# A reordered opening in a two-layer kernel: idle products, moved SiLUs, evictions and decays, and a new spread of the key units

## The chip, the cores and the metric

The kernel runs on one core of one Trainium2 chip. The metric is the device time of one execution in microseconds (us); three runs were taken. The engines are TensorE (PE in the rows), VectorE (DVE), ScalarE (ACT), GpSimd (POOL) and SyncE (SP), which issues most of the transfers.

## The reference, cut to what matters

The reference is a network of two layers on x (4 batches, 512 tokens, width 512) and a context (4, 512, 256). Layer 0 is a selective scan on the context, gated by the normalised x, and then a feed-forward with quantised activations and ternary weights. Layer 1 is cross-attention with 16 heads and a mixture of experts. What this change touches is the scan of batch 0, the ternary weights and the attention's keys:

```python
# the scan (one batch): e = 512 channels, n = 16 states
x  = in_proj_w @ ctx                          # product A
u  = silu(conv4(x) + conv_b)                  # 4-tap convolution along time
dt_lo, Bm, Cm = split(x_proj_w @ u)           # product B
delta = softplus(dt_proj_w @ dt_lo + dt_proj_b)    # product C
for n in range(16):
    state_n[t] = state_n[t-1] * exp(delta[t] * A[:, n]) + delta[t] * u[t] * Bm[n, t]
y  = sum_n state_n * Cm[n] + D * u
out = y * silu(z)                             # z is the normalised x

# ternary weights of the feed-forward
scale = clip(mean(abs(w), axis=-1), 1e-5); w_q = clip(round(w / scale), -1, 1)

# keys of the attention, per head
k = rmsnorm((ctx @ Wk).reshape(B, S, H, D), gk)
```

## The kernel before, in words

Every engine runs a queue of its own in the order of the code, and all waits are semaphores that are written by hand. The program has an opening and then a loop over the four batches ("turns"). Inside a turn the scan of the next batch is interleaved with the feed-forward and the attention of this one, and TensorE is busy nearly throughout. The opening has nothing to interleave with, so it takes in work that belongs to later turns.

**The head of the opening.** `scan_a` makes product A in four parts (TensorE), and ScalarE copies each from PSUM to `xin`. The convolution of channels 0 and 1 is made on TensorE (`scan_conv`) with diagonal matrices that GpSimd builds (`diagonals`), and that of channels 2 and 3 on VectorE (`taps`). ScalarE applies SiLU: `scan_silu` to a bank of PSUM, `summed_silu` to a result of `taps`. `scan_b` and `scan_c` make products B and C. In C's four banks ScalarE reads each twice, once for `Abs` and once for `Identity` with the offset `dt_b`; two banks of PSUM serve the four parts in turn. The softplus then goes back and forth: an exponential and a logarithm on ScalarE, five passes on VectorE (`softplus_start`, `softplus_end`). Ahead of `softplus_start` in VectorE's queue stands `gate_norm`, whose power function is GpSimd's (`rstd`). GpSimd's queue has, in this order, `diagonals(0)`, a `partition_all_reduce` of the gains, and that power.

**The eight rounds.** The 16 states are scanned in eight rounds r of two (i = 0 and 1). In each, VectorE multiplies by B (`times_b`), scans four times (`scans`), then multiplies both states by C (`times_c`), and works out the signs of one block of weights (`ternary(r + 2)`, none in rounds 6 and 7). ScalarE makes the factors exp(delta * A) of the next round, one call of four instructions per state: `decay(0, r + 1, i)`. TensorE adds the results into four banks, `y_sum(r, i)`. `times_b(r + 1, 1)` overwrites what `y_sum(r, 1)` reads and waits for it, and `scans` waits for its decay.

**What fills the rounds.** A key unit n is two heads of the keys of one batch. On TensorE it is `first_k(n, h)` (four products of 512 columns, each two records in the trace) and `first_sums(n, h)` (sums of squares). On ScalarE it is `first_out(n)` (four instructions: two squares, two scaled copies) and `first_sums_out(n, h)`. SyncE loads the next weights and stores the unit (`k_dma`). A ternary block r is `w_sums` (four sums of absolute values, ScalarE), `ternary` (VectorE), `tern` (transposes on TensorE) and `w_out` (five evictions on ScalarE). Units 0 and 1 stand ahead of the rounds (`U_EARLY = 2`), `round_units(r)` gives the units of round r (two in rounds 0 to 4, one in 5 to 7), and unit 15, the first of the turn, stands behind the rounds. `y_first` is the set of banks that `y_sum` adds to; it is begun with D * u (`d_times_u`).

## Time and profile before

| | |
|---|---|
| median of 3 runs | 1937.62 us (1936.42 to 1937.79) |
| the profiled execution's own time | 1934.49 us |
| its span | 1932.8 us |
| TensorE busy | 1797.8 us (93%) |
| VectorE busy | 1206.4 us (62%) |
| ScalarE busy | 1090.6 us (56%) |
| mean granted TensorE clock | 0.970 |

The span runs from the first to the last instruction, so 1.7 us of the profiled execution's time lie outside it. The shares are means over the whole span. The opening takes its first 240 us, and the shares there differ from those of the turns.

### The profile page before, as it was taken

How to read it: one execution, taken by the hardware profiler on the slowest of the kernel's cores; microseconds unless marked ns; L12 is line 12 of the kernel's file. 1: busy time of each engine (PE TensorE's matmuls, PEld its weight loads, DVE VectorE, ACT ScalarE, POOL GpSimd, SP SyncE). 2: the span in 40 equal slices, each digit the busy share in tenths (PEclk: the TensorE clock that was granted, in tenths of full speed). 3: DMA queues.
4: the chain of work that ended last, by engine and by line, in shares of the span. 5: the costliest groups of instructions: out<-in, count | busy, mean ns of one | idle time of the engine just before them, and what ended most of it. 6: DMA issues, size and time to landing. Idle time of an engine off the chain costs nothing.

```text
span 1932.8 us, 26062 instructions
## 1 busy us (share of the span) xinstructions
PE 1797.8 (93%) x8318; PEld 1154.4 (60%) x8319; DVE 1206.4 (62%) x1551; ACT 1090.6 (56%) x2454; POOL 236.1 (12%) x197
## 2 busy tenths in 40 slices
PE   7799899999999999999999999998989999989895
PEld 3455455776765576767655777765567676634442
DVE  5799778877775788777678977783641001144422
ACT  5577447666654676666547666754554554453420
POOL 0002011110100010000102000000031010033032
PEclk9799899999999989999999999999999999999997
DMA  7165222323231122223122323232044323213433
GB/s 213 44 191 189 88 57 66 93 76 94 83 84 61 51 87 89 91 77 102 50 88 66 93 76 103 76 120 77 33 137 90 78 68 85 49 50 108 127 105 124
DMA packets 113862, 175.76 MB, mean 91 GB/s; under 512 B 12400, under 2 KB 65648, under 8 KB 113280
## 3 DMA queue, kind: packets, MB, share of 16 engines
q1 hardware_dynamic: 99136, 158.06, 26.0%
q0 software_dynamic: 13840, 15.21, 3.9%
q10 hardware_dynamic: 816, 1.57, 0.2%
q8 instruction: 42, 0.69, 0.1%
q14 instruction: 28, 0.23, 0.0%
HBM read 146.23 MB, written 34.87 MB: 94 GB/s over the span
## 4 chain that ended last, share of the span: by engine, by line
PE 78%; DVE 9%; ACT 6%; issue 4%; another core or an unknown queue 2%; DMA 1%; POOL 1%; SPq 1%; ACTq 0%; DVEq 0%
PE ps L1942 27%; PE pp L1942 17%; PE px L1942 17%; PE pd L1942 6%; PE po L1942 5%; DVE arena L1469 2%; PE ps L2136 1%; PE pp L2290 1%; DVE arena L1461 1%; ACT hbuf L1235 1%; PE pd L2261 1%; PE po L2261 1%; ACT arena L980 1%; PE px L1994 1%
## 5 line engine op out<-in xcount | busy, mean ns | idle before, releaser
L1469 DVE TENSOR_TENSOR_SCAN arena<-arena 128x512 f32<-128x512 f32 x256 | 292.2, 1204 | 16.3 <-ACT arena L980 15.7
L1235 ACT ACTIVATE hbuf<-ps,shift,rms_k 128x512 f32<-128x512 f32 x256 | 198.4, 777 | 124.3 <-PE ps L1942 117.2
L1942 PE MATMUL ps<-qkT 128*128 128x512 f32 x512 | 250.8, 601 | 7.3 <-ACT hbuf L1235 4.0
L1942 PE MATMUL pp<-wq,xnT 128*128 128x256 f32 x1024 | 233.6, 382 | 0.0
L1942 PEld LDWEIGHTS pp<-wq,xnT 128*128 128x128 f32 x1024 | 191.6, 192 | 24.0
L813 POOL TENSOR_TENSOR rms<-ssv,minus_half 128x4 f32<-128x4 f32 x64 | 80.9, 1264 | 860.5 <-ACT ssv L1211 860.5
L980 ACT ACTIVATE arena<-arena,a_neg 128x512 f32<-128x512 f32 x256 | 163.7, 722 | 0.0
L1942 PEld LDWEIGHTS po<-v_ext,hbuf 128*128 128x128 f32 x768 | 105.9, 191 | 61.2 <-issue 61.2
L1942 PEld LDWEIGHTS ps<-qkT 128*128 128x128 f32 x512 | 82.5, 190 | 84.0 <-ACT hbuf L1235 58.2
L1461 DVE TENSOR_TENSOR arena<-arena,bc 128x2048 f32<-128x2048 f32 x56 | 126.3, 2287 | 6.7 <-issue 5.6
L1942 PE MATMUL px<-wo,oT 128*128 128x512 f32 x256 | 121.8, 596 | 5.9 <-issue 5.9
L1682 DVE TENSOR_TENSOR xc<-xc,px 128x512 f32<-128x512 f32 x64 | 43.1, 677 | 129.7 <-PE px L1942 129.7
L1480 DVE TENSOR_TENSOR arena<-arena,bc 128x2048 f32<-128x2048 f32 x52 | 118.7, 2282 | 0.0
L1942 PE MATMUL ps<-wo,oT 128*128 128x512 f32 x256 | 115.9, 593 | 1.1 <-ACT v_ext L1197 1.1
L1942 PE MATMUL ps<-wv,ctx_att 128*128 128x256 f32 x512 | 115.7, 379 | 0.0
L1229 ACT ACTIVATE qkT<-pp 128x512 f32<-128x512 f32 x64 | 37.9, 597 | 137.0 <-PE pp L2290 137.0
L1487 DVE TENSOR_TENSOR arena<-arena 128x2048 f32<-128x2048 f32 x48 | 110.0, 2292 | 6.5 <-ACT arena L972 3.2
L1942 PE MATMUL pd<-v_ext,hbuf 128*128 128x129 f32 x768 | 106.7, 275 | 0.0
L1942 PE MATMUL po<-v_ext,hbuf 128*128 128x129 f32 x768 | 106.4, 275 | 0.0
L1942 PEld LDWEIGHTS ps<-wv,ctx_att 128*128 128x128 f32 x512 | 97.3, 190 | 13.2
L1942 PE MATMUL pp<-ctx_att,wk 128*128 128x512 f32 x200 | 98.0, 635 | 2.8 <-DMA ctx_att<-in_ctxT 1.8
L1942 PE MATMUL px<-v_ext,hbuf 128*128 128x129 f32 x512 | 99.0, 275 | 0.0
(340 smaller groups left out, 3034.2 us busy)
## 6 DMA issues: line engine op xcount, KB each, us to landing
bc<-bc_dram SPq DMA_DIRECT2D x56, 512.0 KB, 5.4
wo<-in_Wo SPq DMA_DIRECT2D x32, 512.0 KB, 3.6
wq<-in_Wq SPq DMA_DIRECT2D x32, 512.0 KB, 3.5
qkT<-kt_dram SPq DMA_DIRECT2D x32, 512.0 KB, 4.4
hbuf<-in_w SPq DMA_DIRECT2D x8, 1024.0 KB, 10.0
wv<-in_Wv SPq DMA_DIRECT2D x32, 256.0 KB, 2.8
kt_dram<-xnT SPq DMA_DIRECT2D x13, 512.0 KB, 3.0
wk<-in_Wk SPq DMA_DIRECT2D x25, 256.0 KB, 3.3
```

The costliest lines, as they stand in the source:

```text
L813: nc.gpsimd.tensor_tensor(rms[:, j], ssv[:, j], half, ALU.pow).then_inc(rms_done, 1)
L980: nc.scalar.activation(dA[i][:, e], delta[:, e], ACT.Exp, scale=a_neg[:, e, bass.ds(g * GH + i, 1)]).then_inc(exp_done[i], 1)
L1229: nc.scalar.activation(qT[:, h], pp[bank][:], ACT.Copy).then_inc(pp_drained[bank], 1)
L1235: nc.scalar.activation(pT[:, h, k], ps[s_use % 2][:], ACT.Exp, bias=shift[:, 0:1], scale=rms_k[:, bass.ds(G * (GH * NT) + (h * NT + k), 1) ...
L1461: V.tensor_tensor(hb[i], du, bc_i[:, 0:1, :].broadcast_to((P, EC, L)), ALU.mult).then_inc(dbu_done[i], 1)
L1469: V.tensor_tensor_scan(hb[i][:, e], dA[i][:, e], hb[i][:, e], 0.0, ALU.mult, ALU.add).then_inc(scan_done[i], 1)
L1480: V.tensor_tensor(dst, hb[i], bc_i[:, 1:2, :].broadcast_to((P, EC, L)), ALU.mult).then_inc(hc_done[i], 1)
L1487: V.tensor_tensor(u, u, hb[i], ALU.add).then_inc(y_added, 1)
L1682: V.tensor_tensor(xc[:, k], xc[:, k], px[bank][:], ALU.add).then_inc(px_drained[bank], 1)
L1942: return nc.tensor.matmul(out, lhsT, rhs, start=first, stop=last, **kw)
L1994: m = nc.tensor.transpose(bank[:, e * P:(e + 1) * P], u[:, e, k * P:(k + 1) * P], ident[:])
L2261: m = nc.tensor.transpose(o_bank[h][:, k * P:(k + 1) * P], o_rows[:, h, k], ident[:])
```

## The change: what it does

- TensorE runs 14 products of 128 columns whose result nobody reads, ahead of its wait for the first weights (`ip_in`). `conv_w` and `ident` are loaded third and fourth, with a semaphore of their own, `conv_in`, for which GpSimd's diagonals and VectorE's taps wait in place of all constants.
- On ScalarE one SiLU stands ahead of the first set of weight sums and the other three between the two sets.
- The four banks of C are evicted by VectorE, offset added, behind its two ternary blocks; ScalarE takes the absolute value from SBUF, behind the exponential of `a_neg`. VectorE's `gains_set` moves behind the taps.
- Unit 0's evictions stand ahead of `w_out(0)`, its sums behind `decay(0, 0, 0)`; TensorE's order follows. `decay(0, 1, 0)` moves ahead of round 0, and `y_sum(0, 0)` ahead of unit 2's products.
- Rounds 0 and 7 have one key unit, the six between have two. Unit 15 is round 7's, stored from the buffer `wq`, and its part in the first turn is dropped.

```diff
         def round_units(r):
-            first = U_EARLY + r + min(r, R_TWO)
-            return range(first, first + (2 if r < R_TWO else 1))
+            first = U_EARLY + max(0, 2 * r - 1)
+            return range(first, first + (1 if r in (0, TC - 1) else 2))
...
             sp.dma_start(ipT[:], dram["ipT"].rearrange("(c p) e -> p c e", p=P)).then_inc(ip_in, 16)
+            sp.dma_start(conv_w[:], dram["conv_w"].rearrange("(e p) k -> p e k", p=P)).then_inc(conv_in, 16)
+            sp.dma_start(ident[:], dram["ident"]).then_inc(conv_in, 16)
             constants()
...
                 if s == 0:
-                    pool.wait_ge(const_in, 16 * 17)
+                    pool.wait_ge(conv_in, 16 * 2)
...
                     act.wait_ge(full, n)
-                    if s == 0:
-                        nc.scalar.activation(hb[0][:, e], bank, ACT.Abs, bias=dt_b[:, e:e + 1]).then_inc(sp_abs, 1)
                     nc.scalar.activation(delta[:, e], bank, ACT.Identity, bias=dt_b[:, e:e + 1]).then_inc(drained, 1)
+            def first_abs():
+                for e in range(EC):
+                    _, _, drained, n = at(before_turns, ("C", 0), e)
+                    act.wait_ge(drained, n)
+                    nc.scalar.activation(hb[0][:, e], delta[:, e], ACT.Abs).then_inc(sp_abs, 1)
...
-            act.wait_ge(const_in, 16 * 17)
+            act.wait_ge(const_in, 16 * 15)
+            summed_silu(0, range(2, 3))
             tern(w_sums, 0)
+            scan_silu(0, before_turns, range(1))
+            summed_silu(0, range(3, 4))
+            scan_silu(0, before_turns, range(1, 2))
             tern(w_sums, 1)
-            for e in range(2):
-                scan_silu(0, before_turns, range(e, e + 1))
-                summed_silu(0, range(2 + e, 3 + e))
             scan_b(0, before_turns)
-            scan_c(0, before_turns)
+            nc.scalar.activation(a_neg[:], a_neg[:], ACT.Exp).then_inc(a_exp, 1)
+            first_abs()
             softplus_exp(0)
-            nc.scalar.activation(a_neg[:], a_neg[:], ACT.Exp).then_inc(a_exp, 1)
             softplus_ln(0)
+            first_out(0)
             tern(w_out, 0, range(4))
             act.wait_ge(a_ready, 1)
             decay(0, 0, 0)
+            for h in range(GH):
+                first_sums_out(0, h)
             tern(w_out, 1, range(4))
             decay(0, 0, 1)
             d_times_u(0)
             tern(w_sums, 2)
-            for n in range(U_EARLY):
+            for n in range(1, U_EARLY):
                 first_out(n)
                 for h in range(GH):
                     first_sums_out(n, h)
+            decay(0, 1, 0)
...
-                    if r + 1 < TC:
+                    if r + 1 < TC and not r == i == 0:
                         decay(0, r + 1, i)
...
+            dve.wait_ge(conv_in, 16 * 2)
             taps(0, before_turns, range(2, EC))
+            gains_set()
             for r in range(2):
                 ternary(0, r, 1)
+            for e in range(EC):
+                bank, full, drained, n = at(before_turns, ("C", 0), e)
+                dve.wait_ge(full, n)
+                V.tensor_scalar(delta[:, e], bank, dt_b[:, e:e + 1], None, ALU.add).then_inc(drained, 1)
             shift_set()
             gate_norm(0, 0)
...
+            pe.wait_ge(const_set, 1)
+            for _ in range(14):
+                mm(pd[:, 0:P], ones[:], ones[:], True, True)
+            pe.wait_ge(ip_in, 16)
...
-            for r in range(2):
-                tern(r, range(4))
-            first_sums(0, 0)
-            for n in range(1, U_EARLY):
-                first_k(n, 0)
-                first_sums(n - 1, 1)
-                first_k(n, 1)
-                first_sums(n, 0)
+            tern(0, range(4))
+            for h in range(GH):
+                first_sums(0, h)
+            tern(1, range(4))
+            for h in range(GH):
+                first_k(1, h)
             pe.wait_ge(ud_done, EC)
             for e in range(EC):
                 mm(y_first[e][:], ident[:], u[:, e], True, True)
-            first_sums(U_EARLY - 1, 1)
+            for h in range(GH):
+                first_sums(1, h)
             for r in range(TC):
                 units = round_units(r)
+                if r == 0:
+                    y_sum(r, 0)
                 for h in range(GH):
                     first_k(units[0], h)
-                y_sum(r, 0)
+                if r:
+                    y_sum(r, 0)
...
-            n0 = unit_at(0, 0)[0]
-            k_turned(n0, 0, B - 1, 0)
-            k_turned(n0, 0, B - 1, 1)
-            k_sums(n0, 0, k_sq_turn, 0)
...
                     scan_a(b + 1, turn_, 0)
-                    kss(0, 1)
+                    if b:
+                        kss(0, 1)
                     scan_a(b + 1, turn_, 1)
```

The first place is the head of ScalarE's queue, behind the four copies of product A; `qk_raw,w_sum<-hbuf` are the weight sums, `arena<-ps,conv_b` and `arena<-arena,conv_b` the SiLUs. Before:

```order
L998 ACTIVATE qk_raw,w_sum<-hbuf 128x512 [waits abs_done,stage_in0,const_in]
L998 ACTIVATE qk_raw,w_sum<-hbuf 128x512 [waits abs_done] x3
L998 ACTIVATE qk_raw,w_sum<-hbuf 128x512 [waits abs_done,stage_in1]
L998 ACTIVATE qk_raw,w_sum<-hbuf 128x512 [waits abs_done] x3
L923 ACT_TABLE_LOAD
L923 ACTIVATE arena<-ps,conv_b 128x512 [waits py_full0]
L929 ACTIVATE arena<-arena,conv_b 128x512 [waits taps_done]
L923 ACTIVATE arena<-ps,conv_b 128x512 [waits py_full1]
L929 ACTIVATE arena<-arena,conv_b 128x512 [waits taps_done]
```

Of the change, at the same place:

```order
L932 ACT_TABLE_LOAD [waits taps_done]
L932 ACTIVATE arena<-arena,conv_b 128x512 [waits const_in]
L1006 ACTIVATE qk_raw,w_sum<-hbuf 128x512 [waits abs_done,stage_in0]
L1006 ACTIVATE qk_raw,w_sum<-hbuf 128x512 [waits abs_done] x3
L926 ACTIVATE arena<-ps,conv_b 128x512 [waits py_full0]
L932 ACTIVATE arena<-arena,conv_b 128x512 [waits taps_done]
L926 ACTIVATE arena<-ps,conv_b 128x512 [waits py_full1]
L1006 ACTIVATE qk_raw,w_sum<-hbuf 128x512 [waits abs_done,stage_in1]
L1006 ACTIVATE qk_raw,w_sum<-hbuf 128x512 [waits abs_done] x3
```

The last SiLU now stands ahead of the second set of sums, and the table load carries the wait for the first tap sums.

The second place is ScalarE's queue around the beginning of round 0: `ssv_k<-pp,eps` are unit 1's sums, `dsum<-pp` and `wo<-pp,kgain` unit 2's evictions, `arena<-arena,a_neg` the decays of round 1. Before:

```order
L1042 ACTIVATE ssv_k<-pp,eps 128x4 [waits pp_full0]
L1042 ACTIVATE ssv_k<-pp,eps 128x4 [waits pp_full1]
L1029 ACTIVATE dsum<-pp 128x512 [waits pp_full0]
L1034 ACTIVATE wo<-pp,kgain 128x512 [waits k_stored0]
L1029 ACTIVATE dsum<-pp 128x512 [waits pp_full1]
L1034 ACTIVATE wo<-pp,kgain 128x512
L980 ACTIVATE arena<-arena,a_neg 128x512 [waits scan_done0]
```

Of the change:

```order
L1050 ACTIVATE ssv_k<-pp,eps 128x4 [waits pp_full0]
L1050 ACTIVATE ssv_k<-pp,eps 128x4 [waits pp_full1]
L988 ACTIVATE arena<-arena,a_neg 128x512 [waits scan_done0]
L988 ACTIVATE arena<-arena,a_neg 128x512 x3
L1037 ACTIVATE dsum<-pp 128x512 [waits pp_full0]
L1042 ACTIVATE wo<-pp,kgain 128x512 [waits k_stored0]
L1037 ACTIVATE dsum<-pp 128x512 [waits pp_full1]
```

The four instructions of `decay(0, 1, 0)` now stand ahead of unit 2's evictions.

The third place is TensorE's queue there: `arena,ident` into ps, po and pd begins `y_first`, `ones,dsum` are unit 1's sums, `ctx_att,wk` unit 2's products, `xc,ident` is `y_sum(0, 0)`. Before:

```order
L1942 MATMUL pd<-arena,ident 128x512
L1942 MATMUL pp<-ones,dsum 128x1 [waits k_squares,pp_drained1]
L1942 MATMUL pp<-ones,dsum 128x1 x3
L1942 MATMUL pp<-ctx_att,wk 128x512 [waits pp_drained0,wk_in,ctx_att_in]
L1942 MATMUL pp<-ctx_att,wk 128x512
L1942 MATMUL pp<-ctx_att,wk 128x512 [waits pp_drained1,wk_in,ctx_att_in]
L1942 MATMUL pp<-ctx_att,wk 128x512
L1942 MATMUL ps<-xc,ident 128x512 [waits hc_done0]
```

Of the change:

```order
L1962 MATMUL pp<-ones,dsum 128x1 [waits k_squares,pp_drained1]
L1962 MATMUL pp<-ones,dsum 128x1 x3
L1962 MATMUL ps<-xc,ident 128x512 [waits hc_done0]
L1962 MATMUL ps<-xc,ident 128x512
L1962 MATMUL po<-xc,ident 128x512
L1962 MATMUL pd<-xc,ident 128x512
L1962 MATMUL pp<-ctx_att,wk 128x512 [waits pp_drained0,wk_in,ctx_att_in]
```

`y_sum(0, 0)` has gone ahead of unit 2's products.

## Rows read from the trace of the kernel before

**Rows 1.** Windows of the opening: length, each engine's busy time, granted TensorE clock, DMA

```profile
50.00:108.00 58.00, 45.02 (x188) 27.00 (x189) 43.19 (x45) 36.55 (x77) 0.00 (x0) 0.81 0.27 79
108.00:230.00 122.00, 107.79 (x501) 61.79 (x500) 118.93 (x88) 79.55 (x143) 13.69 (x2) 0.95 0.47 153
```

**Rows 2.** Timeline, round 1 (start, length, engine, line, instruction, idle before)

```profile
71.80 2.29 DVE L1461 TENSOR_TENSOR arena<-arena,xnT 128x2048 f32<-128x2048 f32 x1 [0.22 <-DVE qkT L1429]
...
85.34 2.55 ACT L980 ACTIVATE arena<-arena,a_neg 128x512 f32<-128x512 f32 x4
...
86.16 4.57 DVE L1469 TENSOR_TENSOR_SCAN arena<-arena 128x512 f32<-128x512 f32 x4 [12.07 <-ACT arena L980]
92.11 2.29 DVE L1461 TENSOR_TENSOR arena<-arena,xnT 128x2048 f32<-128x2048 f32 x1 [1.37 <-PE pd L1942]
...
104.08 0.17 DVE L1422 TENSOR_SCALAR w_scale<-w_sum 128x4 f32<-128x4 f32 x1 [0.69 <-ACT qk_raw L998]
```

**Rows 3.** The chain that ended last, head of the opening: start, length, what

```profile
19.08 2.56 ACT qk_raw L998 x8
...
22.96 0.69 ACT arena L923
25.70 3.62 PE ps L1942 x16
29.84 1.11 PE ps L1942 x2
...
37.26 1.92 ACT arena L960
```

**Rows 4.** Timeline of VectorE, head of the opening and round 0

```profile
15.44 2.32 DVE L1555 SCALAR_TENSOR_TENSOR arena<-arena,conv_w 128x511 f32<-128x511 f32 x3
...
24.32 0.17 DVE L1422 TENSOR_SCALAR w_scale<-w_sum 128x4 f32<-128x4 f32 x1 [0.22 <-DVE qkT L1429]
...
28.41 2.46 DVE L1490 BATCH_NORM_STATS2 ln_st<-xs 128x6 f32<-128x512 f32 x4
...
39.28 1.23 DVE L1438 TENSOR_SCALAR arena<-arena 128x2048 f32<-128x2048 f32 x1 [4.48 <-ACT arena L960]
...
49.91 2.29 DVE L1461 TENSOR_TENSOR arena<-arena,bc 128x2048 f32<-128x2048 f32 x1
...
63.52 2.27 DVE L1480 TENSOR_TENSOR xc<-arena,bc 128x2048 f32<-128x2048 f32 x1
```

**Rows 5.** Timeline: product A, GpSimd's three operations, a later wait for its power

```profile
6.06 9.30 PE L1942 MATMUL ps<-dsum,ipT 128*128 128x512 f32 x16 [6.06 <-DMA ipT<-in_ipT]
...
12.91 1.90 POOL L797 TENSOR_TENSOR bc<-ident,conv_w 128x1024 f32<-128x1024 f32 x1 [11.75 <-DMA gains<-in_gk]
...
24.45 0.38 POOL L802 PARTITION_ALL_REDUCE gains<-gains  x1 [9.64 <-issue]
...
33.55 1.05 POOL L807 TENSOR_TENSOR ln_r<-ln_ve,minus_half 128x4 f32<-128x4 f32 x1 [8.73 <-issue]
...
250.44 0.21 DVE L1502 SCALAR_TENSOR_TENSOR ln_nm<-ln_mv,ln_r 128x4 f32<-128x4 f32 x1 [1.12 <-POOL ln_r L807]
```

**Rows 6.** Timeline, ScalarE's first key eviction

```profile
62.66 0.57 ACT L1029 ACTIVATE dsum<-pp 128x512 f32<-128x512 f32 x1
```

**Rows 7.** Timeline, end of the rounds and beginning of the first turn

```profile
218.07 2.29 DVE L1461 TENSOR_TENSOR arena<-arena,xnT 128x2048 f32<-128x2048 f32 x1 [0.88 <-PE pd L1942]
...
227.21 3.78 PE L1942 MATMUL ps<-xc,ident 128*128 128x512 f32 x4 [4.92 <-DVE xc L1480]
...
237.89 1.29 DVE L1541 TENSOR_TENSOR arena<-ps,hbuf 128x512 f32<-128x512 f32 x2 [8.54 <-PE pd L1942]
238.40 3.68 PE L1942 MATMUL pp<-ctx_att,wk 128*128 128x512 f32 x8
...
243.40 1.28 DVE L1563 TENSOR_TENSOR xs<-xs,px 128x512 f32<-128x512 f32 x2 [3.02 <-PE px L1994]
```

**Rows 8.** Transfers issued in 225 to 262 us: size, median us to landing

```profile
dsum<-in_ctxT ACTq DMA_DIRECT2D x1, 512.0 KB, 3.5
```

More of the change, by code:

```diff
@@ L304, in program @@
         const_in = sem("const_in")
+        conv_in = sem("conv_in")
         ip_in = sem("ip_in")
@@ L501, in first_unit @@
         def first_unit(n):
-            return n, FIRST_BATCHES[n // G_FIRST] * NG + n % G_FIRST
+            return n, G_FIRST if n == U_FIRST else FIRST_BATCHES[n // G_FIRST] * NG + n % G_FIRST
         def stored_by(end, parity):
@@ L546, in _ @@
         def _(sp):
-            small = [(ident, dram["ident"]), (ident_bf, dram["ident_bf"]), (minus_bf, dram["minus_bf"]), (tri, dram["tri"]),
-                     (conv_w, dram["conv_w"].rearrange("(e p) k -> p e k", p=P)),
+            small = [(ident_bf, dram["ident_bf"]), (minus_bf, dram["minus_bf"]), (tri, dram["tri"]),
                      (a_neg, dram["A_log"].rearrange("(e p) n -> p e n", p=P)),
@@ L647, in _ @@
             for i in range(2):
-                sp.wait_ge(k_stored[i], stored_by(U_FIRST, i))
+                sp.wait_ge(k_stored[i], stored_by(U_FIRST + 1, i))
             wo_load(0)
@@ L658, in unit_dma @@
                     k_dma(n, G, b * NG, stage, g_next)
-                unit_dma(0, k_stage_turn[0])
+                if b:
+                    unit_dma(0, k_stage_turn[0])
                 if scan:
@@ L1133, in turn @@
                     scan_a(b + 1, turn_, 0)
-                    kss_out(0, 1)
+                    if b:
+                        kss_out(0, 1)
                     scan_a(b + 1, turn_, 1)
@@ L1399, in _, with gains_set @@
             V = nc.vector
-            dve.wait_ge(const_in, 16 * 17)
-            V.tensor_tensor(kgain[:], gains[:, 0:1], gains[:, 1:2], ALU.mult).then_inc(gain_step, 1)
-            dve.wait_ge(gain_step, 1)
-            V.scalar_tensor_tensor(gains[:, 2:3], kgain[:], -1.0, kgain[:], ALU.mult, ALU.max).then_inc(gain_step, 1)
-            dve.wait_ge(gain_step, 2)
-            V.tensor_scalar(kgain[:], kgain[:], SCALE, None, ALU.mult).then_inc(gain_step, 1)
+            def gains_set():
+                dve.wait_ge(const_in, 16 * 15)
+                V.tensor_tensor(kgain[:], gains[:, 0:1], gains[:, 1:2], ALU.mult).then_inc(gain_step, 1)
+                dve.wait_ge(gain_step, 1)
+                V.scalar_tensor_tensor(gains[:, 2:3], kgain[:], -1.0, kgain[:], ALU.mult, ALU.max).then_inc(gain_step, 1)
+                dve.wait_ge(gain_step, 2)
+                V.tensor_scalar(kgain[:], kgain[:], SCALE, None, ALU.mult).then_inc(gain_step, 1)
             def shift_set():
@@ L1995, in scan_end @@
                     m.then_inc(full, 1)
-            pe.wait_ge(ip_in, 16)
             def y_sum(g, i):
@@ L2067, in first_k @@
             def first_k(n, h):
-                k_turned(n, 0, n // G_FIRST + 1, h)
+                k_turned(n, 0, min(n // G_FIRST + 1, B - 1), h)
             def first_sums(n, h):
@@ L2175, in turn @@
                     scan_a(b + 1, turn_, 0)
-                    kss(0, 1)
+                    if b:
+                        kss(0, 1)
                     scan_a(b + 1, turn_, 1)
```

9 lines of the change are left out of this document (4 added, 5 removed).

## The prediction, made before the result was known

> **What bounds the kernel now.** I read the windows first, to see which engine fills which stretch. From 108 to 230 us VectorE is busy 118.93 of 122 us: these rounds are as long as VectorE's work. From 50 to 108 us it is busy only 43.19 of 58 us, and TensorE's mean granted clock is 0.81 [rows 1]. So the rounds' beginning has a hole of some 15 us in the engine that sets their length. The timeline says where: in round 1 VectorE waits 12.07 us for ScalarE's decays, 1.37 us for a bank that TensorE reads, and 0.69 us for weight sums [rows 2]. ScalarE is not short of time there. Its decay of 2.55 us [rows 2] stands in its queue behind unit 2's evictions, those wait for unit 2's products, and these stand on TensorE behind units 0 and 1 and the start of `y_first`.
>
> Ahead of round 0 the chain of waits alternates between the engines: weight sums, SiLU, product B, product C, exponential [rows 3]; VectorE waits 4.48 us for the exponential and begins `softplus_start` at 39.28 and round 0 at 49.91 [rows 4]. Behind round 7 VectorE waits 8.54 us for TensorE, whose `y_sum` ran its first four records in 3.78 us where eight records of the same shape take 3.68 us later; it then waits 3.02 us more while TensorE makes unit 15's products [rows 7]. The first is the lower clock level, 1.2 GHz, against 2.4 GHz. All of this is opening. The turns behind it are TensorE's and I take them to shift as a whole.
>
> **The head, worked out.** Product A has 16 records in 9.30 us [rows 5]; all at the full level they take twice 3.68, about 7.2 us with one tail. If the idle products raise the clock by 6.1 us, A ends at 13.3 in place of 15.4. The 14 products have a quarter of the columns: 0.23 us each at the full level, 0.47 at the half (a quarter of 2 x 3.78/4), so 6.6 us if none is fast; begun in the first microsecond they hold A back by 1.5 us at most. I take none.
>
> The third part of A is then on hand at 12.0. Channel 2's taps need about 0.5 us and 2.32 us [rows 4]: 14.9. The table load (the 1.3 us between the end of the sums at 21.64 and the SiLU at 22.96) and one SiLU of 0.69 [rows 3] end at 16.9, the first sums (2.56) at 19.5, three SiLUs at 21.5. So product B begins at 21.5 in place of 25.70, and the second sums (2.56) run beside it. C followed B's beginning by 4.1 us (29.84) [rows 3]: 25.6.
>
> VectorE's second ternary block begins when those sums end, at 24.1, and lasts 3.8 us (24.32 to the 28.41 of the statistics, less 0.25 for the shift) [rows 4]: 27.9. Then come the four evictions, which this trace does not show on VectorE. The nearest row is two reads of PSUM of that size in 1.29 us [rows 7], so 0.6 each; from below 0.48, if they cost what the first tap does. I take 0.6, as both read PSUM. The third must also wait for its product, 1.11 us for two records [rows 3], of which 0.6 is covered: 2.9 us, to 30.8. Shift 0.25, statistics 2.46, small steps 0.6: 34.1. GpSimd's power costs VectorE 1.12 us in the turn [rows 5], and 0.2 follows: `softplus_start` at 35.5, **3.8 us earlier**. ScalarE is ready before: absolute value at 31.5, exponential of 1.92 [rows 3] at 33.4. So VectorE's and not ScalarE's queue sets this, and 2.1 us is the most that cheaper evictions could add.
>
> GpSimd starts the all-reduce 9.64 us after the diagonals' end and the power 8.73 us after the all-reduce, with its inputs there for most of that [rows 5]. The diagonals now start between conv_w's landing and 12.91, the time before. Even at 12.91 the power is possible at 33.6, below my 34.1. But then the convolution starts at 14.8 and not 13.3, which puts SiLU and product B 1.3 us later; I take an early start, and keep 1.3 for the range.
>
> **Round 0 to round 1.** Round 0 begins at 46.1. ScalarE reached unit 0's evictions 15.1 us after the softplus' third pass (62.66, against 49.91 less 2.3) [rows 4, 6]; the same list without them, plus two sums of 0.16, ends at 43.8 + 15.4 = 59.2. Unit 1's four evictions end at 61.4, its sums about 62.4, `decay(0, 1, 0)` at 65.0. VectorE needs it at 74.1 - 3.8 = 70.3. The 12.07 us go, with 5 us to spare.
>
> What is late next is TensorE. `y_first` can begin at 56.7 (59.2 less the sums' 2.56). At the full level eight records issue in 3.5 us and a unit's sums in 0.8 per head: `y_first` to 60.2, unit 1's sums to 61.8, `y_sum(0, 0)` (its input is there at 63.52 + 2.27 - 3.8 = 62.0 [rows 4]) to 65.5, unit 2 to 69.0, one sum, `y_sum(0, 1)` to 73.3. VectorE wants that bank at 92.11 - 1.37 - 12.07 - 3.8 = 74.9 [rows 2]. So the 1.37 us go too, by a margin of 1.6. The weight sums of block 3 now end at about 81 for a need at 86: 0.69 goes. Together **14.1 us**. The key unit taken from round 0 costs nothing in rounds 5 and 6: rounds 2 to 4 held two units beside the same VectorE work without a wait.
>
> **The end of the rounds.** With two units in rounds 5 and 6 TensorE's gaps shrink, so I take the full level: the 0.88 us wait of round 7 goes, and from 227.21 it is 3.5 + 0.8 + 3.5 us to the end of `y_sum(7, 1)`, 235.1 in place of 237.89: **0.9 and 2.8 us** [rows 7]. With unit 15 gone from here, the transposes follow the gate (2.5 us for its four parts) and VectorE starts 0.7 us behind it and not 3.0: **2.3 us**. The dropped `kss(0, 1)` is 0.8 us of TensorE's work ahead of `in_quant`, where TensorE is last: **0.8 us**. Against this stands one transfer. The context of the next scan uses the buffer of unit 15's squares, so it is issued behind unit 15's sums, 1 us behind the gate's start, takes 3.5 us [rows 8], and is wanted at 5.0; beside the loads of Wo and Wq it can be up to 1 us late. I take 0.3.
>
> Sum: 3.8 + 14.1 + 0.9 + 2.8 + 2.3 + 0.8 - 0.3 = 24.4 us. The profiled execution (1932.8 of span, 1934.49 in all) becomes 1910.1. It lies 3.1 below the median, so the median of runs becomes 1937.6 - 24.4 = **1913.2 us**.
>
> **Rivals.**
>
> *TensorE's clock stays low into round 0 (0.08).* All the terms after 56.7 at half speed: `y_first` to 63.7, sums 67.1, `y_sum` 74, unit 2 81, `y_sum(0, 1)` 89.4. VectorE then waits 14.5 us in round 1 and the hole has only moved: gain 9.9, time 1927.7. For it: the mean clock of 0.81 there [rows 1]. Against it: unit 1's products now run directly behind `tern(1)`, and TensorE has nearly continuous work from 52 us. If the clock rises on the way, the wait is 0 to 5 us. The Trainium skill, TensorE: Matmul & The Clock Gate, HAM oscillation, says that waits between groups of products drop the clock and that each next group then begins slow; by that rule TensorE's wait for ScalarE before `y_first` brings this rival's time. The 3.78 us of rows 7 behind a wait of 4.92 us agree with it.
>
> *The head gives nothing (0.09).* The idle products don't raise the clock in time, or the evictions queue behind ternary work as long as ScalarE's did: 3.8 us less, 1917.0. For it: VectorE's queue ahead of `softplus_start` has grown by 2.9 us and only its earlier start pays for it. The same page (What's actually happening) says that the moment of the rise varies from run to run; by that the 14 products could be too few, and product A would start 1.5 us late at worst. No row here shows such products.
>
> *Slower (0.03): TensorE becomes the bound of the rounds.* A round with two units and a ternary block is some 20 us of TensorE's work at the full level (two units of 5.1, `y_sum` 7.0, transposes 2.5), beside VectorE's 21. At the half level it is 39, so every round spent at 1.2 GHz adds 18 us in `times_b(r + 1, 1)`. From 1.4 such rounds on the gain is used up; two give 1937.6 - 24.4 + 36 = 1949. Against it: in 108 to 230 us the mean granted clock was 0.95 with more gaps than now [rows 1].
>
> *It doesn't do what it says (0.02):* the turns swallow the shift, 1937. Nothing in the turns is tied to absolute time, so I give it little.
>
> **Chances and range.** The forecast gets 0.78. Its own lower end is 2.1 for cheaper evictions and 1.5 for the scatter of runs: 1909.5. Its upper end has 1.3 (diagonals), 1.5 (idle products), up to 5 (TensorE in round 1), 2.8 (end at half speed) and 0.7 (context); all at once give 1924.5, and I stop at 1923. That includes the second rival. A measurement of this kernel tells some 0.2% (3.9 us) from no change. Faster by more: 0.95; within: 0.02; slower: 0.03.
>
> **What would show each step.** Records of product A 0.43 us apart from the first; product B at 21.5; `softplus_start` at 35.5, waiting for GpSimd's power; round 0 at 46.1; no wait before round 1's scans; round 2 at 90.0 instead of 107.97; gate about 25 us earlier, and no key product between the gate and the transposes. The prediction is wrong if VectorE waits for TensorE's bank in round 1, if a round behind it is longer than 21.1 us, or if ScalarE's or GpSimd's part holds `softplus_start` past 37.

## The result, and the profile after

The changed kernel took 1914.42 us (median of 4 runs, 1909.75 to 1918.54), the kernel before on the same chip 1937.02 us (4 runs, 1936.08 to 1937.79): ratio 0.9886, 95% interval 0.9867 to 0.9904. The forecast was 1913.2. Its profiled execution took 1917.8 us, the slower end of its four, with a span of 1916.1, which is 16.7 us less than the profiled one of before. The experiments ran later on other chips, where the kernel before takes 1914 us. They are compared by their ratio to it.

The windows of the opening answer to [rows 1]; columns as there.

```profile
50.00:108.00 58.00, 51.44 (x237) 29.58 (x238) 57.23 (x56) 40.89 (x84) 0.00 (x0) 0.92 0.37 110
108.00:210.00 102.00, 96.16 (x455) 55.92 (x454) 100.52 (x77) 70.35 (x129) 13.45 (x1) 1.00 0.50 160
```

The hole is closed: VectorE is busy 57.23 of 58 us where it was 43.19, and behind that the rounds are as full of VectorE's work as before. The timeline of the head, TensorE and GpSimd, answers to [rows 3, 5]:

```profile
1.10 5.20 PE L1962 MATMUL pd<-ones 128*128 128x128 f32 x28 [1.10 <-POOL minus_magic L787]
6.20 7.13 PE L1962 MATMUL ps<-dsum,ipT 128*128 128x512 f32 x16
...
6.76 1.90 POOL L800 TENSOR_TENSOR bc<-ident,conv_w 128x1024 f32<-128x1024 f32 x1 [5.59 <-DMA ident<-in_ident]
...
21.89 3.62 PE L1962 MATMUL ps<-arena,xpT 128*48 128x256 f32 x16 [1.71 <-ACT arena L926]
```

Product A takes 7.13 us and not 9.30 and B starts at 21.89, both within 0.4 us of the prediction; the early start of the diagonals that it took, without naming a time, is there (6.76). Behind B the plan breaks. VectorE, the evictions of C to round 1, answers to [rows 2, 4]:

```profile
27.85 1.41 DVE L1588 TENSOR_SCALAR arena<-ps,dt_b 128x512 f32<-128x512 f32 x2 [0.16 <-DVE v_ext L1443]
30.65 0.75 DVE L1588 TENSOR_SCALAR arena<-ps,dt_b 128x512 f32<-128x512 f32 x1 [1.39 <-PE ps L1962]
32.36 0.75 DVE L1588 TENSOR_SCALAR arena<-ps,dt_b 128x512 f32<-128x512 f32 x1 [0.95 <-PE ps L1962]
...
37.81 1.23 DVE L1452 TENSOR_SCALAR arena<-arena 128x2048 f32<-128x2048 f32 x1
...
72.65 4.57 DVE L1483 TENSOR_TENSOR_SCAN arena<-arena 128x512 f32<-128x512 f32 x4
77.14 2.27 DVE L1475 TENSOR_TENSOR arena<-arena,xnT 128x2048 f32<-128x2048 f32 x1
...
92.20 2.29 DVE L1475 TENSOR_TENSOR arena<-arena,bc 128x2048 f32<-128x2048 f32 x1 [0.21 <-DVE v_ext L1443]
```

The evictions cost 0.7 each and wait 2.3 us for TensorE's products, so they end at 33.1 and not 30.8; `softplus_start` begins at 37.81. But round 1 has no wait: the scans at 72.65 and `times_b` at 77.14 follow their predecessors at once. Round 2 begins at 92.20 instead of 107.97. The end of the rounds answers to [rows 7]:

```profile
211.26 1.88 PE L1962 MATMUL ps<-xc,ident 128*128 128x512 f32 x4
...
219.32 1.29 DVE L1555 TENSOR_TENSOR arena<-ps,hbuf 128x512 f32<-128x512 f32 x2 [6.73 <-PE pd L1962]
...
222.06 1.06 PE L2014 MATMUL px<-ident,arena 128*128 128x128 f32 x8 [2.10 <-DVE arena L1555]
...
222.72 1.28 DVE L1577 TENSOR_TENSOR xs<-xs,px 128x512 f32<-128x512 f32 x2 [0.92 <-PE px L2014]
...
223.47 1.97 PE L2014 MATMUL px<-ident,arena 128*128 128x128 f32 x8 [0.34 <-DVE xs L1577]
225.23 7.81 PE L1962 MATMUL ps<-dsum,ipT 128*128 128x512 f32 x16
```

`y_sum(7, 0)` now runs at the full level (four records in 1.88 us, 3.78 before), and the waits of 8.54 and 3.02 us became 6.73 and 0.92. New is the wait of 2.10 us on TensorE behind the gate: in the transposes that follow, eight take 1.06 us and the next eight 1.97.

**The lead, place by place.** A landmark is the first record of `scan_a` (`ps<-dsum,ipT`) or of the Q products (`pp<-wq,xnT`) of a turn; the row before minus the row after is the lead. Between the profiled executions it was 20.0 us at `scan_a` of turn 0 (245.24 and 225.23), 14.9 at its Q products (322.03 and 307.15) and 15.8 at those of turn 3 (1418.18 and 1402.37). So some 5 us of what the opening won were gone 80 us later. (Leads of the experiments are against the same execution of before, though on other chips. That can be done up to the end of the turns: e4, the kernel before with one small edit, trails that execution by 4.0 us at `scan_a` of turn 0 and by 3.8 at the Q products of turn 3. The 19 us by which its chip is faster arise only behind 1862 us.) The windows of TensorE's granted clock in the first turn say where, of the kernel after and then of before at the same work:

```profile
268.00:280.00 12.00, 11.78 (x39) 5.85 (x40) 7.19 (x11) 5.39 (x8) 0.00 (x0) 0.72 0.07 28
300.00:312.00 12.00, 10.97 (x44) 9.74 (x45) 11.77 (x9) 4.44 (x9) 0.00 (x0) 0.58 0.46 152
```

```profile
288.00:300.00 12.00, 11.70 (x51) 5.49 (x51) 9.63 (x15) 6.75 (x9) 2.23 (x2) 1.00 0.06 24
320.00:332.00 12.00, 12.00 (x66) 10.84 (x66) 11.76 (x7) 9.26 (x33) 2.85 (x2) 1.00 0.37 126
```

### The profile page after: what moved, and what is told of

Read it like the earlier page. It is cut to its first block, busy times and chain, and to the rows that moved or that the text cites. A ratio compares the mean times of both kernels' runs of the same rounds, so it can differ in the third digit from the quotient of the medians.

```text
span 1916.1 us, 26089 instructions
## 1 busy us (share of the span) xinstructions
PE 1801.8 (94%) x8314; PEld 1162.0 (61%) x8347; DVE 1207.7 (63%) x1555; ACT 1089.6 (57%) x2450; POOL 235.6 (12%) x197
## 3 DMA queue, kind: packets, MB, share of 16 engines
q1 hardware_dynamic: 99136, 158.06, 26.2%
## 4 chain that ended last, share of the span: by engine, by line
PE 78%; DVE 11%; ACT 5%; issue 4%; another core or an unknown queue 2%; POOL 1%; DMA 0%; ACTq 0%; DVEq 0%; SPq 0%; POOLq 0%
PE ps L1962 27%; PE px L1962 17%; PE pp L1962 17%; PE pd L1962 6%; PE po L1962 5%; DVE arena L1483 3%; DVE arena L1475 2%; PE ps L2157 2%; PE pp L2312 1%; ACT hbuf L1247 1%; PE pd L2283 1%; PE po L2283 1%; DVE arena L1494 1%; DVE ln_st L1504 1%
```

## The experiments

Each kernel was executed four or five times, e4 ten and e6 eleven times. Beside the ratio stand landmarks of the one profiled execution, which can be a fast or a slow one of its kernel; where that matters its own time is given. The ratio is that of the record with its 95% interval, and it is not simply the quotient of the medians printed beside it.

**e1, the changed kernel again.** No edit.

> The changed kernel again. Its four runs lie in two groups, 1909.8 and 1911.0, and 1917.8 and 1918.5, where the four of before lie within 1.7 us. Theory: in some executions TensorE's clock falls twice in the first turn (269 to 279 and 303 to 311 us of the profiled one, granted 0.50, about 7 us of lost lead), in others it does not; then this profile has either a lead of 20 us over before that is kept to the end and a time near 1910, or falls as before and a time near 1918. Rival: the 7 us are lost in every execution and the spread has another place, such as the opening; then a run near 1910 has a smaller lead loss in the opening and the same falls in the first turn.

1894.93 us (1888.43, 1894.84, 1895.02, 1896.14), ratio 0.9906 (0.9891 to 0.9921). The profiled run is the one of 1888.43. Its opening is that of the first profile (`softplus_start` 37.58, gate 219.12), but at 300 us TensorE kept the full level. The two profiles of one kernel at the same four steps, first the run of 1917.8, then that of 1888.43:

```profile
300.62 1.11 PE L2254 MATMUL ps<-ident,hbuf 128*128 128x128 f32 x8 [1.88 <-DVE hbuf L1527]
302.14 1.94 PE L2254 MATMUL ps<-ident,hbuf 128*128 128x128 f32 x8 [0.41 <-ACT xnT L1202]
303.88 3.41 PE L1962 MATMUL pp<-ones,qk_raw 128*128 128x1 f32 x16
307.15 9.60 PE L1962 MATMUL pp<-wq,xnT 128*128 128x256 f32 x32
```

```profile
298.83 1.11 PE L2254 MATMUL ps<-ident,hbuf 128*128 128x128 f32 x8 [1.88 <-DVE hbuf L1527]
300.35 1.12 PE L2254 MATMUL ps<-ident,hbuf 128*128 128x128 f32 x8 [0.40 <-ACT xnT L1202]
301.30 1.84 PE L1962 MATMUL pp<-ones,qk_raw 128*128 128x1 f32 x16
303.01 7.15 PE L1962 MATMUL pp<-wq,xnT 128*128 128x256 f32 x32
```

The lead at the Q products of turn 3 is 22.5 us here and was 15.8. The first fall is shorter too (0.86 in 268 to 280 us). The first four runs of the changed kernel also fall into two pairs, 1909.75 and 1911.04, 1917.8 and 1918.54. So this kernel has two outcomes some 7 us apart, and at least one place that decides between them is a clock that falls, or not, behind a wait of TensorE of 1.88 us. All twelve profiles without idle products at this place, of whichever kernel, have this wait in the first turn (1.88 to 1.91 us). The second eight transposes behind it took 1.94 us in six of the profiles and 1.11 or 1.12 in five; in e6 the trace has all sixteen as one entry, of 3.60 us.

**e2, without the idle products.**

```
-            for _ in range(14):
-                mm(pd[:, 0:P], ones[:], ones[:], True, True)
```

> The changed kernel without its 14 idle products. Theory: product A has its first 4 us at half speed again, ends about 2 us later (15.3 for 13.3) and softplus_start, whose chain runs through A, the SiLUs and product B, comes 1.5 to 2 us later: about 1.8 us slower than the changed kernel. Rival: the chain runs through the weight sums, whose data land at about 16 us, and the products give nothing: 0 us.

1896.55 us, ratio 0.9910 (0.9897 to 0.9924). In the profile product B begins at 24.72 and not 21.84, `softplus_start` at 39.78 and not 37.58, `scan_a` at 228.84 and not 224.87. The idle products win 2.2 us of the head. The other 1.8 us at `scan_a` are mostly round 7's key unit, whose products took 5.37 us here and 3.67 in e1; in e3, e7 and e9, which have the idle products, they took 5.33 to 5.37 too. In the time nothing of it is to be seen (1.6 us between the medians), as runs scatter by 7.

**e3, product C evicted by ScalarE**, as before the change, the exponential of `a_neg` ahead of it.

```
-            for e in range(EC):
-                bank, full, drained, n = at(before_turns, ("C", 0), e)
-                dve.wait_ge(full, n)
-                V.tensor_scalar(delta[:, e], bank, dt_b[:, e:e + 1], None, ALU.add).then_inc(drained, 1)
...
-            first_abs()
+            scan_c(0, before_turns)
```

> The changed kernel with C's four banks evicted by ScalarE as before (two readings each), the exponential of a_neg still ahead of them. Theory: in the changed kernel VectorE's queue (evictions to 33.0, layer norm to 37.8) sets softplus_start, so the evictions on VectorE cost: with them on ScalarE the layer norm ends at about 32 and ScalarE's exponential at about 33.7 to 34, so softplus_start comes at about 34 in place of 37.81, and the kernel is 3 to 4 us faster. Rival: ScalarE's two readings per bank hold product C back as much as VectorE's queue did, softplus_start at 37 or later, no gain.

1887.17 us, ratio 0.9861 (0.9846 to 0.9876). `softplus_start` began at 35.80, 1.8 to 2.0 us earlier than with VectorE's evictions. Moving the offsets to VectorE was a loss. At `scan_a` the lead was 20.4 us, no more than e1's: TensorE fell to the half level late in the rounds and the gate waited 8.4 us for it. Round 7's products, first in e1, then here:

```profile
207.55 3.67 PE L1962 MATMUL pp<-ctx_att,wk 128*128 128x512 f32 x8 [0.66 <-issue]
```

```profile
205.70 5.33 PE L1960 MATMUL pp<-ctx_att,wk 128*128 128x512 f32 x8 [0.60 <-issue]
```

The kernel is faster than the changed one by more than the intervals, by 7.8 us between the medians. But the profiled run is the slow one of its four (1894.64 us, the others 1885.47 to 1887.80), so the profile shows 1.8 to 2.0 us of this in the head and not where the rest comes from.

**e4, of the change the moved decay alone**, on the kernel before.

```
+            decay(0, 1, 0)
...
-                    if r + 1 < TC:
+                    if r + 1 < TC and not r == i == 0:
                         decay(0, r + 1, i)
```

> The kernel before with only decay(0, 1, 0) moved ahead of round 0. Theory: TensorE's order is as before, y_sum(0, 1) still ends at about 92, and VectorE waits there instead: the 12.07 us split into some 8 us ahead of the scans and the rest at the bank, round 2 still begins at 107.9 and the time stays within 1 us of before. Rival: the decay was the cause by itself and the kernel gains 10 us or more.

1914.86 us, ratio 1.0004 (0.9995 to 1.0014): nothing. VectorE's two waits in round 1 (all starts are some 4 us later than in before, by a slower product B in the head, of which more below):

```profile
85.77 4.57 DVE L1470 TENSOR_TENSOR_SCAN arena<-arena 128x512 f32<-128x512 f32 x4 [7.44 <-ACT arena L980]
96.17 2.29 DVE L1462 TENSOR_TENSOR arena<-arena,xnT 128x2048 f32<-128x2048 f32 x1 [5.83 <-PE pd L1943]
```

12.07 + 1.37 us became 7.44 + 5.83: the wait moved to the bank. The decay's place was the last link of the hole, and TensorE's queue the next.

**e8, the middle alone**, on the kernel before: units 0 and 1, `y_sum(0, 0)` and `decay(0, 1, 0)` in the new order on TensorE and ScalarE. The cut shows TensorE's main part; ScalarE's lines are those of the diff.

```
-            for r in range(2):
-                tern(r, range(4))
-            first_sums(0, 0)
-            for n in range(1, U_EARLY):
-                first_k(n, 0)
-                first_sums(n - 1, 1)
-                first_k(n, 1)
-                first_sums(n, 0)
+            tern(0, range(4))
+            for h in range(GH):
+                first_sums(0, h)
+            tern(1, range(4))
+            for h in range(GH):
+                first_k(1, h)
```

> The kernel before with only the order of units 0 and 1, of y_sum(0, 0) and of decay(0, 1, 0) changed, on ScalarE and TensorE; the head ahead of the softplus and the spread of the key units are those of before. My term for this was 14.1 us (12.07 + 1.37 + 0.69). Moving the decay alone gave nothing, for VectorE then waited 7.4 us for it and 5.8 us for TensorE's bank. Theory: TensorE's order is the other half, and together they give 12 to 14 us: ratio 0.9925 to 0.994, and VectorE's waits in round 1 under 2 us in sum. Rival: without the earlier head and one key unit fewer in round 0 TensorE is still late by several us: ratio 0.995 to 0.998.

1899.46 us (1898.85 to 1900.69), ratio 0.9924 (0.9910 to 0.9937), 14.9 us faster. VectorE has no wait over 0.22 us in round 1. From `softplus_start` to the first `times_b` of round 2 it took 54.5 us (41.12 to 95.64), in before 68.7 and in the changed kernel 54.4.

**e6, the spread of the key units alone**, on the kernel before.

```
-            first = U_EARLY + r + min(r, R_TWO)
-            return range(first, first + (2 if r < R_TWO else 1))
+            first = U_EARLY + max(0, 2 * r - 1)
+            return range(first, first + (1 if r in (0, TC - 1) else 2))
```

> The kernel before with only the key units spread anew (one in rounds 0 and 7, two in rounds 1 to 6, unit 15 taken from behind round 7, the dropped key sum in the first turn). My terms for this part were 0.9 (bank wait of round 7) + 2.8 (y_sum at the full clock) + 2.3 (unit 15 gone) + 0.8 (sum dropped) - 0.3 = 6.5 us, and up to 1.4 more if one unit fewer in round 0 also takes the bank wait of round 1. In the changed kernel the lead grew by only 4.3 us from round 2 (15.8) to in_quant (20.1). Theory: the terms hold but for the fall of the clock behind the gate, which is new there: ratio 0.9965 to 0.998 (4 to 6.5 us faster). Rival: a TensorE that is idle behind the gate gives back what the unit took: within 2 us of the kernel before.

1911.65 us (11 runs), ratio 0.9985 (0.9976 to 0.9994): 2.9 us and not 6.5. VectorE ended its last `times_c` at 227.76 (before 229.35), but the gate was at 237.46 (before 237.89), as TensorE came late to `y_sum(7, 0)`:

```profile
222.86 6.70 PE L1942 MATMUL pp<-ctx_att,wk 128*128 128x512 f32 x8 [0.54 <-issue]
229.40 1.88 PE L1942 MATMUL ps<-xc,ident 128*128 128x512 f32 x4
```

From the gate to VectorE's first `xs` it took 3.4 us and not 5.5, from there to `in_quant` 15.55 and not 16.45. These are the 2.3 and the 0.8 of the prediction, as 2.1 and 0.9. The terms up to the gate were 0.4 together: at the half level the products of round 7's unit took 6.70 us and stood in front of `y_sum`, whose input was there at 225.55; with 3.68 us they would have held it only until 226.4. What was left went again in the turns: at turn 0's Q products the lead was -0.6 us (the clock fell at product C, 284 to 292 us).

**e7, `y_sum(0, 0)` back behind unit 2's products**, in the changed kernel. The edit is the last piece of the diff of TensorE's order, undone.

> The changed kernel with y_sum(0, 0) put back behind unit 2's products. Theory: it costs nothing, as y_sum(0, 1) ends at the same time and VectorE wanted that bank 1.2 us after its end: within 0.2% of the changed kernel (ratio 0.990 to 0.992 to the kernel before), no wait of VectorE ahead of round 1's second times_b over 0.3 us. Rival: TensorE waits for unit 2's squares in front of it and loses the clock in rounds 0 and 1: round 2 begins 1 to 4 us later.

1894.45 us, ratio 0.9889 (0.9867 to 0.9912), against e1's 0.9906, and no wait over 0.21 us in round 1. No gain of this move can be seen.

**e5, product C with 128 rows.** The changed kernel; C is made differently, in the opening and in every turn, by 112 more rows of zeros in `dtT`. With it come two fills by GpSimd, and `dtT` is loaded last, behind them.

```
-        dtT = sb("dtT", [DR, DI])
+        dtT = sb("dtT", [P, DI])
...
+        dlo_all = dA[1][:, 0]
...
+            nc.gpsimd.memset(dtT[:], 0.0).then_inc(pad_set, 1)
+            nc.gpsimd.memset(dlo_all, 0.0).then_inc(pad_set, 1)
...
-                    mm(bank, dtT[:, e * P:(e + 1) * P], dlo[:], True, True).then_inc(full, 1)
+                    mm(bank, dtT[:, e * P:(e + 1) * P], dlo_all, True, True).then_inc(full, 1)
```

> The changed kernel with one thing different: product C (dtT by dlo, four records of 16 rows by 512 columns) is made with all 128 rows, 112 of them zero in dtT, so each record has the same columns and the same result, and only more of the array is in use. In the profiles of the changed kernel the granted clock falls to 0.50 to 0.55 while product C runs or right behind it: 28 to 36 us, 268 to 280 us, and again near 636 in the next turn; behind each of them the records take twice their time. Theory: it is the idle rows of product C that let the clock fall. Then the stretches 28:36 and 268:280 show 1.00, VectorE's evictions of C end 1.5 to 2 us earlier (31 us and not 33), softplus_start begins at 36 to 37 us and not 37.6, and the whole is 5 to 10 us faster than the changed kernel (1884 to 1890 on a chip where that takes 1895). Rival: rows of zeros count for nothing, or the fall has to do with something else (the transposes and the waits around it): the same stretches stay at 0.5 to 0.9, the time is within 2 us of the changed kernel's (0.9906 of the kernel before).

1887.79 us, ratio 0.9843 (0.9820 to 0.9867), where e1 has 0.9906. TensorE in the head, first e1, then e5:

```profile
25.97 1.95 PE L1962 MATMUL ps<-arena,dtT 16*128 16x512 f32 x4 [0.51 <-issue]
28.60 3.49 PE L1962 MATMUL ps<-arena,dtT 16*128 16x512 f32 x4 [0.67 <-DVE arena L1588]
32.01 5.54 PE L1962 MATMUL pp<-ctx_att,wk 128*128 128x512 f32 x8
```

```profile
26.15 1.95 PE L1969 MATMUL ps<-arena,dtT 128*128 128x512 f32 x4 [0.52 <-issue]
28.78 1.98 PE L1969 MATMUL ps<-arena,dtT 128*128 128x512 f32 x4 [0.67 <-DVE arena L1595]
30.60 3.60 PE L1969 MATMUL pp<-ctx_att,wk 128*128 128x512 f32 x8
```

With the same waits and columns around them, the third and fourth parts took 1.98 us in place of 3.49, and unit 0's eight records behind them 3.60 in place of 5.54. `softplus_start` began at 36.26. The fall at 268 us was gone as well (1.00), that at 296 us was not. The other profiles bear this out. In the head the second pair took 2.36 to 3.78 us and unit 0's products 5.09 to 6.59 in all nine without padding, 1.98 to 2.28 and 3.60 in all five with it. In the first three turns product C took over 4 us at 9 of 27 places without padding and 3.78 or 3.79 at all 15 with it.

**e11, the same padding on the kernel before.**

> The kernel before with product C padded to 128 rows, and nothing of the change. Theory: the fall of the clock at product C in the first turn is new with the change (before has 1.00 in 288:300), so here only the head gains (product C ran in 28 to 36 us with 0.79 and 0.78) and a turn or two behind it: 0 to 4 us faster (ratio 0.998 to 1.000). Rival: padding is worth the same here as there, 12 us (0.994), and then e5's gain over the changed kernel says nothing of what the change lost.

1902.13 us (1901.76 to 1904.48), ratio 0.9940 (0.9927 to 0.9954). The rival held: by the ratios the padding is worth some 12 us in either kernel (by the medians 12.5 us here and 7.1 in the changed kernel, whose runs lie in two groups), so e5's gain does not measure what the change lost. In this profile the lead is 0 at 322 us and comes later: 4.0 us at the Q products of turn 1, 5.9 of turn 2, 6.3 of turn 3. Before has a fall at the steps of e1's two fences, but in turn 1 (676 to 688 us at 0.93, 0.50, 0.50); with the padding it is gone there. Those 6.3 us are not the whole gain, as the profiled execution of before was one with a fast head. Against e4's profile, of the same chip and with the slower head, the lead is 3.6 us at `scan_a` of turn 0 and 3.8, 8.0, 9.8 and 10.0 us at the Q products of turns 0 to 3, of 10.7 between the two executions. So some 4 us come from the opening and 4 from the fall in turn 1; the 1.8 between turns 1 and 2 stay open.

**e9, e5 with idle products ahead of two waits**, the one behind the gate and the one of 1.88 us.

```
+            def idle(turn_, seg, n):
+                bank, _ = use(turn_, (seg, 0), 0)
+                for _ in range(n):
+                    mm(bank[:, 0:P], ones[:], ones[:], True, True)
+
             def scan_end(s, turn_):
+                idle(turn_, "POST", 8 if s == 0 else 5)
...
                 def xn_turned():
+                    idle(turn_, "AP", 7)
```

> The kernel of e5_padded_c with idle products (ones by ones, 128 columns, 0.23 us each) on TensorE at two places of every turn where its trace shows TensorE waiting and the granted clock falling behind the wait: 8 (5 behind the first turn) ahead of the transposes of scan_end (idle 2.1 us behind the gate, then 220:228 at 0.85 and 0.72; 584 at 0.58; 940 at 0.88 and 0.70; 1300 at 0.68 and 0.50), and 7 ahead of the transposes of the second layer norm (idle 1.88 us, then 296:308 at 0.74, 0.50, 0.50, with 16 products of one column in 3.41 us). Theory: what costs there is the idle time ahead and not the kind of the products behind: the clock stays at 1.00 in 220:228 and 296:308, in_quant comes 0.5 to 1 us earlier and the turn 4 to 6 us shorter by 310 us: together 5 to 9 us faster than e5 (ratio 0.9795 to 0.982). Rival: the products are begun before the wait and are over before its end, or the one-column products let the clock fall by themselves: no change over 0.1% against e5 (0.9843), or slower where the 1.2 to 1.9 us of products outlast the wait.

1881.91 us (1880.98 to 1886.11), 5.9 less than e5's median, though the ratios are the same, 0.9844 (0.9828 to 0.9859) and 0.9843. At both places the clock did what the theory said: 1.00 in 220 to 228 us, where e5 has 0.85 and 0.72, and at the second place this, on TensorE:

```profile
293.82 1.72 PE L1969 MATMUL ps<-ones 128*128 128x128 f32 x14
295.89 1.11 PE L2269 MATMUL ps<-ident,hbuf 128*128 128x128 f32 x8 [0.35 <-DVE hbuf L1534]
297.41 1.12 PE L2269 MATMUL ps<-ident,hbuf 128*128 128x128 f32 x8 [0.40 <-ACT xnT L1209]
298.37 1.84 PE L1969 MATMUL pp<-ones,qk_raw 128*128 128x1 f32 x16
300.07 7.15 PE L1969 MATMUL pp<-wq,xnT 128*128 128x256 f32 x32
```

One-column products run in 1.84 us here, so they do not bring the fall by themselves. At this place the level stayed in all three turns of e9 and of e12 that were compared (1.12 us for the second eight transposes). The lead over the kernel before at the Q products is 22.0, 26.2, 28.0 and 29.6 us in turns 0 to 3; in e5 it is 18.9, 21.3, 23.1 and 23.3. In the profile it gains 6 us, within the intervals of the runs nothing can be told from e5.

**e10 and e12, the padded C evicted by ScalarE, without and with the idle products of e9.** Edits as in e3, e5 and e9.

> The kernel of e5_padded_c with product C evicted by ScalarE, as in before, and the exponential of a_neg ahead of it (that is, e3_c_on_act with the padded product C). In e3 VectorE waited 3.1 us for ScalarE's exponential and began softplus_start at 35.80, with the third and fourth records of C at the half clock; in e5 the same records took 1.98 in place of 3.49 us. Theory: VectorE's four evictions and the rest of its queue hold softplus_start in e5 (36.26), ScalarE's would end 1.5 us earlier with C at the full clock: softplus_start at 34.0 to 34.5, ratio 0.9825 to 0.984. Rival: ScalarE's own evictions and absolute values are the longer queue whatever the clock: softplus_start at 35.5 to 36.3 and the time within 1 us of e5 (0.9843).

> The kernel of e10_padded_c_on_act (product C padded and evicted by ScalarE) with the idle products of e9_padded_fill at both places. At the Q products of the last turn the profiled run of e9 was 29.6 us ahead of the kernel before, that of e10 26.3, that of e5 23.3, and of the changed kernel 15.8 and 22.5 in its two profiled runs. Theory: the two parts are apart, 2.1 us in the opening and some 6 us in the turns, and add up: 31 to 32 us ahead, median 1878 to 1881 on a chip where the kernel before takes 1914 (ratio 0.981 to 0.983), and runs that scatter less than the 8 to 10 us of e5 and e10, as the place at 296 us where two runs of one kernel differed is at the full clock in all of them. Rival: the phase of everything behind the opening moves by 2.1 us and the clock falls elsewhere: no better than e9 (1881.9, mean ratio 0.9844).

e10: `softplus_start` at 34.14, 2.1 us before e5's, as the theory said; 1886.3 us, ratio 0.9848 (0.9826 to 0.9869), not told apart from e5. e12: `softplus_start` at 35.11, lead 30.8 us at the Q products of turn 3, 1883.12 us (1880.26 to 1883.77), ratio 0.9837 (0.9823 to 0.9850). That is the best of the ratios, and 0.7% better than e1's; against e5, e9 and e10 the intervals overlap. Its runs lie within 3.5 us of each other.

## Why the prediction was right, and where it was not

That the hole in round 1 is the main gain, and how it closes, was right. That the total came out within 1.2 us is in part luck. Between the profiled executions the opening gave 20.1 us where 24.4 were worked out, the turns took some 5 of them, and 16.7 us are left at the end. The medians lie 22.6 us apart all the same, because the profiled run of before is 2.5 us below its median and that of after 3.4 above its own, which falls between two pairs of runs. By the terms, each as a difference between the two profiled executions (start times, and for `times_c` its end: 39.28, 107.97, 229.35, 237.89, 243.40, 259.85 before; 37.81, 92.20, 212.59, 219.32, 222.72, 239.72 after):

| from, to | predicted | measured |
|---|---|---|
| start to `softplus_start` | 3.8 | 1.5 |
| to round 2 | 14.1 | 14.3 |
| to VectorE's last `times_c` | 0.9 | 1.0 |
| to the gate | 2.8 | 1.8 |
| to the first `xs` | 2.3 | 2.1 |
| to `in_quant` | 0.5 | -0.6 |
| sum | 24.4 | 20.1 |

- **Round 0 to round 1** carried the forecast, and e8 shows it by itself: 14.2 us in the profile and 14.9 in the time (0.9924). Of its parts, the new order of units 0 and 1 was needed as much as the decay (e4), and `y_sum(0, 0)` was not (e7). The rival of the low clock did not come: `y_first` began at 59.19 for a predicted 56.7, as late as the head was, but ran at the full level, and `y_sum(0, 1)` ended at 76.1 for a bank wanted at 77.14. The margin of 1.6 us was one of 1.0.
- **The head** was mis-sized in one step, the four evictions. Up to the end of the second ternary block (27.85 for a predicted 27.9) all was as worked out, so the idle products and the early diagonals did what was forecast; e2 and the row at 6.76 bear it out. The step took the third part of C as waiting 0.5 us for a product at the full level. The level fell behind the first pair of products (0.70 in 28 to 30 us, then 0.50), and the second pair took 3.67 us for 1.95. With the level kept (e5) the evictions end at 31.5 and `softplus_start` is at 36.26: so 1.5 of the 2.3 us were the clock, and 0.7 the price of an eviction (0.7 to 0.75, I had taken 0.6). `softplus_start` passed the 37 us that the prediction named as a sign of being wrong, but by VectorE's evictions, not by ScalarE's or GpSimd's part. The choice of ScalarE's or VectorE's queue was judged rightly as VectorE's, but e10's 34.14 shows that ScalarE could have evicted C sooner than VectorE.
- **What the head was measured against** also had luck in it. In the kernel before, TensorE waits some 3 us for the SiLUs ahead of product B, and the level behind this wait is not the same in each execution. The five profiles with that head (before, e4, e6, e8, e11) have 3.62, 6.42, 3.62, 4.97 and 6.52 us for B; against e4's `softplus_start` at 43.52 the changed head is 5.7 us earlier and not 1.5. With the new order of the SiLUs the wait is 1.7 us and B took 3.62 us in all nine profiles, also without the idle products (e2). B before, in e4 and after:

```profile
25.70 3.62 PE L1942 MATMUL ps<-arena,xpT 128*48 128x256 f32 x16 [3.49 <-ACT arena L929]
```

```profile
25.72 6.42 PE L1943 MATMUL ps<-arena,xpT 128*48 128x256 f32 x16 [3.24 <-ACT arena L929]
```

```profile
21.89 3.62 PE L1962 MATMUL ps<-arena,xpT 128*48 128x256 f32 x16 [1.71 <-ACT arena L926]
```

- **The end of the rounds.** VectorE's start behind the gate and the dropped sum hold by e6 (2.1 and 0.9). `y_sum(7, 0)` began 0.9 us behind VectorE's first `times_c`, as unit 15's products stood ahead of it, which is the 1.0 missing at the gate. Even this term depends on the run: the gate waited 6.7 us in five of the nine profiles with the changed opening (after, e1, e5, e10, e12) and 8.4 in the four whose key unit of round 7 fell to the half level (e2, e3, e7, e9). What I left out is the 2.10 us of idle TensorE ahead of the transposes: the second eight took 1.97 us and product A 7.81, where e9, with the wait filled, has 1.25 and 7.03. Here too the fall does not come each time, as e6 and e7 have 1.25 and 7.03 with the same wait. The context's transfer (3.6 us to landing) was waited for nowhere.
- **The turns do not shift as a whole**, as I had it. The clock falls at other places: 0.72 and 0.58 in the first turn where before has 1.00, and before has its own fall in turn 1. Between two runs of one kernel this is 7 us. The Trainium skill, TensorE: Matmul & The Clock Gate, HAM oscillation, says that waits between groups of products drop the clock, each time, in a kernel that waits longer, for its transfers. Behind the 1.88 us wait the first profile agrees (3.41 us for the one-column products), and e1, with the same wait and 1.84 us, shows that here it is not so each time.

## What to carry to other kernels

When a hole is bounded by one late operation, look for what is late next on the other engines before moving it: the decay alone gained nothing, the decay and the new order of the units together 15 us. A stretch that is only moved in time can run at another clock, so follow a lead through the turns landmark by landmark before adding it to the end. One profile is one draw: look at the same place in several before pricing it, the profile of before included. And where thin products (16 rows here) or a wait of TensorE stand among others, filling them cost no time here and removed the falls at those places. Falls at other places stayed.

## What was not expected of the hardware

- Product C with 16 rows and with 128 rows, the same columns: in the head 3.49 against 1.98 us for the second pair, granted clock in 28 to 36 us 0.57 against 1.00, and by the ratios some 12 us of the whole, in both kernels (0.9906 to 0.9843, and 1 to 0.9940).
- Runs of one kernel on one chip fall into two groups 7 to 9 us apart (e5: 1879.7 twice, 1887.8 to 1888.7 three times); with idle products at two waits the spread was 3.5 to 5 us (e12, e9).
- VectorE reads a bank of PSUM of 512 columns with an offset in 0.75 us.
- In before GpSimd's all-reduce started 9.64 us behind the diagonals' end with its input there for all that time (8.77 to 10.07 us in e4, e6, e8 and e11). What fills the gap, no run here tells. In the changed kernel it is 9.73 us too, but there the input came only 0.1 us before the start, so this one says nothing of the gap.
